# Four rotary layers as one looped program, the next layer's first sequences prepared inside the feed-forward

## The reference, cut to what matters

```python
h = x
for l in range(4):
    xn = _ln(h, ln1_w[l], ln1_b[l])
    q, k, v = heads(xn @ Wq.T + bq), heads(xn @ Wk.T + bk), heads(xn @ Wv.T + bv)
    scores = q @ k.T + rel_shift((q + u) @ pos_emb.T)     # causal mask, times 8 ** -0.5
    h = h + (softmax(scores) @ v) @ Wo.T + bo
    fn = _ln(h, ln2_w[l], ln2_b[l])
    h = h + gelu(fn @ W1.T + b1) @ W2.T + b2              # width 512
```

## Time and profile before

| | us |
|---|---|
| median of 3 runs | 6182.86 (6177.51 to 6191.35) |
| the profiled execution | 6190.3 |
| its span | 6188.5 |
| stage of the four rotary layers, within it | about 2000 to 4732 |

### The profile page before, as it was taken

One profiled execution on the slowest core, in us unless ns is written; L12 is line 12 of the kernel. 1 busy time (PEld: TensorE's weight loads), 2 busy tenths in 40 slices (PEclk: granted clock), 3 DMA queues, 4 the chain that ended last, 5 costly groups with the idle time before them and its releaser, 6 DMA issues. The chain is left out here.

```text
span 6188.5 us, 120583 instructions
## 1 busy us (share of the span) xinstructions
PE 5556.4 (90%) x37438; PEld 3444.4 (56%) x37453; DVE 4189.1 (68%) x9588; ACT 2812.6 (45%) x4608; POOL 2250.4 (36%) x3177
## 2 busy tenths in 40 slices
PE   7997999999998799879988999879988879995677
PEld 5664444444443577547764677447754446644564
DVE  6785666666665788458863788358855866677764
ACT  4553222222222355535554455535555655543444
POOL 5661000000000566236641666246632532253312
PEclk9998999999999899989999999989999989997899
DMA  4332232223223566136530666046520000000002
GB/s 133 106 104 98 97 98 95 95 98 98 94 96 91 149 160 157 40 86 160 157 102 18 160 159 158 9 118 159 157 71 5 0 7 0 0 1 4 0 2 63
DMA packets 526330, 527.02 MB, mean 85 GB/s; under 512 B 55698, under 2 KB 436705, under 8 KB 503780
## 3 DMA queue, kind: packets, MB, share of 16 engines
q1 hardware_dynamic: 517684, 517.90, 30.0%
q10 hardware_dynamic: 8320, 5.25, 0.4%
HBM read 337.88 MB, written 185.07 MB: 85 GB/s over the span
## 5 line engine op out<-in xcount | busy, mean ns | idle before, releaser
L362 DVE TENSOR_REDUCE a_mx<-a_unit 128x2 f32<-128x512 f32 (+1 forms) x1920 | 1291.0, 690 | 413.8 <-PE a_unit L564 407.6
L468 ACT ACTIVATE a_prob<-a_slot 128x1536 f32<-128x1536 f32 x640 | 928.5, 1451 | 643.4 <-PE a_slot L587 505.5
L562 PE MATMUL a_unit<-a_sk,a_sq 96*128 96x256 bf16 (+3 forms) x5120 | 744.9, 249 | 80.3 <-DMA a_sk<-a_kscratch 43.7
L1177 ACT ACTIVATE f_silu<-f_pG 128x512 f32<-128x512 f32 x528 | 314.7, 597 | 937.1 <-PE f_pG L1252 923.1
L564 PE MATMUL a_unit<-a_maskq,identb 128*128 128x256 bf16 (+1 forms) x1920 | 601.7, 313 | 0.0
L1119 DVE TENSOR_TENSOR f_gated<-f_spread,f_silu 128x512 f32<-128x512 f32 x512 | 354.5, 692 | 352.9 <-ACT f_silu L1177 308.7
L1229 PE MATMUL f_pO<-f_hidden,f_wd 128*128 128x512 f32 x1056 | 545.9, 599 | 14.5 <-DVE f_hidden L1121 14.1
L1252 PE MATMUL f_pG<-f_xnT,f_wg 128*128 128x512 f32 x1056 | 542.1, 595 | 0.0
L1256 PE MATMUL f_pU<-f_xnT,f_wu 128*128 128x512 f32 x1056 | 540.7, 594 | 0.0
L562 PEld LDWEIGHTS a_unit<-a_sk,a_sq 96*128 96x128 bf16 (+1 forms) x5120 | 383.7, 98 | 279.4 <-DVE a_mx L362 155.4
L306 POOL TENSOR_SCALAR_AFFINE_SELECT a_prob<-a_prob 128x512 f32<-128x512 f32 x480 | 309.5, 645 | 579.7 <-ACT a_prob L468 564.1
(11 more groups left out here) (413 smaller groups left out, 11144.1 us busy)
## 6 DMA issues: line engine op xcount, KB each, us to landing
f_spread<-f_scratch SPq DMA_DIRECT2D x1024, 128.0 KB, 2.9
a_sq<-a_qscratch SPq DMA_DIRECT2D x128, 768.0 KB, 5.8
a_sk<-a_kscratch SPq DMA_DIRECT2D x160, 384.0 KB, 6.6
a_qscratch<-a_parts SPq DMA_DIRECT2D x288, 192.0 KB, 2.2
a_qscratch<-a_parts SPq DMA_DIRECT2D x288, 128.0 KB, 2.2
a_kscratch<-a_parts SPq DMA_DIRECT2D x160, 192.0 KB, 2.4
a_kscratch<-a_parts SPq DMA_DIRECT2D x160, 128.0 KB, 2.2
a_qscratch<-a_parts SPq DMA_DIRECT2D x288, 64.0 KB, 1.8
```

Of the source, the lines that this page charges most:

```text
L362: v.tensor_reduce(dst, src, op=ALU.max, axis=AX.X, negate=True).then_inc(red_done, 1)
L468: act.activation(prob[gr % 2][:, :], slot[:, :], ACT.Exp, scale=SCALE).then_inc(exp_done, 1)
L562: pe.matmul(bank[:, at * wide:(at + 1) * wide], q, sk[b][0:KM, gr * GH + h, 0:wide], start=(at == 0), stop=False)
L1177: act.activation(silu[c % 2][:, :], pG[c % 2][:, :], ACT.Silu).then_inc(silu_done, 1)
```

## The change

```diff
+    EARLY = {6 + 2 * (n + 5): n for n in range(-5, 0)}
+        pH = [slot[:, c * BLK:(c + 1) * BLK] for c in (0, 1, 2, 1)]
+        pT, pO, pR = unit[0], [unit[1], pctx], ring[0]
...
+    # SyncE
+                attn_weights(0)
+                kept.load(sp, core)
+                feed_weights(0)
+                early_steps()
+                with sp.Fori(1, layers) as following:
+                    main_steps(sp, step)
+                    sp.wait_ge(attn_fresh, 1)
+                    attn_weights(following)
+                    early_steps()
+                    sp.wait_ge(feed_fresh, 1)
+                    feed_weights(following)
+                main_steps(sp, step)
...
+    # GpSimd
+                def feed(following):
+                    for s in range(0, BLOCKS + 1):
+                        if following and s - 2 in EARLY and EARLY[s - 2] > -5:
+                            n = EARLY[s - 2]
+                            gather(n, n // 4, n % 4)
+                            split(n, n % 4)
+                        feed_scale(s)
+                        if following and s == 2:
+                            g.wait_ge(op_taken, SEQS)
+                            g.wait_ge(r_pe, 1)
+                            for x in k.sems:
+                                g.sem_clear(x)
+                            g.sem_inc(attn_fresh, 1)
...
+                    if following:
+                        g.wait_ge(r_taken, BLOCKS)
+                        g.wait_ge(m_pe, 1)
+                        for x in f.sems:
+                            g.sem_clear(x)
+                        g.sem_inc(feed_fresh, 1)
...
+    # VectorE, a round of the feed-forward
+                        feed_norm(s)
+                        if following and s - 1 in EARLY:
+                            norm(EARLY[s - 1])
+                        if s < BLOCKS or not following:
+                            feed_add(s)
+                        v.drain()
+                        feed_measure(s)
...
+                            measure(EARLY[s])
+                        if following and s - 1 in EARLY:
+                            rotate(EARLY[s - 1])
...
+    # ScalarE, step 32
+                    if once(n, SEQS):
+                        act.activation(warm[:, :], core["ident"][:, 0:1], ACT.Gelu)
...
+    # TensorE, a step
+                    maxima(0)
+                    if behind_feed and once(n, -2):
+                        turn_back(BLOCKS)
+                    values(n - 1, (j + 1) % 2, 3)
+                    if once(n, SEQS):
+                        widen(-1, 0)
...
+                    if once(n, SEQS - 1):
+                        pe.wait_ge(red_done, SEQS * UNITS)
+                        pe.wait_ge(w_in, W_IN)
+                        feed_turn(-2)
...
+    # TensorE, a round of the feed-forward
+                        for c in range(CH):
+                            narrow(s, c)
+                            widen(s, c)
+                            if c == 1 and (s < BLOCKS or not following):
+                                turn_back(s)
+                            if c == 1 and following and s in EARLY and EARLY[s] > -5:
+                                turn_rows(EARLY[s])
+                            if c == 2:
+                                feed_turn(s)
+                            if c == 2 and following and s - 1 in EARLY and EARLY[s - 1] > -5:
+                                project_turned(EARLY[s - 1], EARLY[s - 1] % 4)
+                            if c == 3 and following and s in EARLY and EARLY[s] > -5:
+                                project(EARLY[s], EARLY[s] % 4)
```

More of the change, by code:

```diff
@@ L2688, in stage_a1 @@
         kept = Kept(nc, stack, "a1_", True)
[L2689 to L2700, removed]
+        rotary_layers(nc, core, "a1_", core["h"], 1e-6, part_of(a, "a1_"), part_of(a, "f1_"), 4, kept)
         kept.held.clear()
```

685 lines of the change are left out of this document (added).

## The result

The changed kernel takes 6046.7 us (median of 4 runs, 6040.8 to 6048.7), the one before 6183.5 us (4 runs, 6177.5 to 6191.4): ratio 0.9776, 95% interval 0.976 to 0.9793. 6028 was forecast, with a range of 6003 to 6078. Its profiled execution took 6047.05 us, with a span of 6045.3: 143.2 us less than before, where 154.7 were forecast.

The account below looks back on a forecast made before the run. TensorE, busy 90% of the span, bounds the kernel; only the joins, 261 us, leave room. Gains of 107.6 and 52.4 less 3 and 2.3 make 154.7 us, so 6182.9 falls to 6028, range 6003 to 6078.

Parts of the forecast that it names:

- Join from feed-forward to attention: Three joins of 65.0 us: clear, meeting and four sequences' serial start leave; 107.6 us gained, feed-forward's growth and branches included.
- The open steps: Steps -2 and -1 between feed-forward and attention, reduced to 24 units of maxima, still open on the path: 20.0 us.
- The taken branch: Layer loop's branch back between step -1 and step 0, taken twice: 0 to 3.6 us each, 2 assumed.
- Feed-forward: First three layers' feed-forwards take in four sequences' products, 7.8 us more: 127.2 us without TensorE idle time; fourth 119.4.
- The first rival: Feed-forward stretched by its sequences, GpSimd's slack being thin: another 3 us for each of twelve, 6064 us; chance 0.12.
- Join from attention to feed-forward: Four joins of 16.6 us go, 3.5 each comes back in steps 30 to 32: 52.4 us gained.
- step 30's 0.9: Attention's step 30: VectorE's statistics stand ahead of the maxima's parts that TensorE waits for, costing 0.9 us.
- First layer: Start of first layer: four sequences strictly one after another, then 24 units; first scores at about 2076, 3 us lost.
- Second rival: Attention's four-step loop begins to pay for its branch: 16 turns, 51 us, time 6079 us; chance 0.06.
- Third: Rival: early sequences don't overlap in the feed-forward at all; 206 us come back, 6234 us, slower than before; chance 0.03.
- Fourth: Rival: a wait keeps the first maxima back until the fill is as long as now; 6131 us; chance 0.03.
- The likeliest case's own range: 6003 to 6052 us, from bounds on open steps, branches, joins behind attention and start, combined as independent; forecast's chance 0.74.

Follow-up runs that it names:

- the loop of eight: Changed kernel with attention's four-step loop (five passes) made an eight-step loop (two passes), four more steps written out behind it: 6078.4 us, ratio 0.9827 to the kernel before.
- the repeat: The changed kernel timed and profiled once more, no code difference: 6045.0 us, ratio 0.9767 to the kernel before.
- its experiment: Changed kernel with the statistics of the feed-forward's first block moved behind the maxima's parts in attention's step 30: 6033.0 us, ratio 0.9756 to the kernel before.

## Why the prediction was right, point by point

**Join from feed-forward to attention: right, 107.4 us against 107.6, with two errors that cancel.** The open steps were put at 20.0, between the floor of 16.5 (VectorE's reductions) and the ceiling of 26.5. They take 17.0: without norms and rotations nothing but the 24 reductions is left (0.68 us each, where 0.64 was read), so the floor was the estimate to take. That is 9 us too little gain in the forecast. The taken branch was put at 2 us of an open 0 to 3.6. It is 6.6 and 6.3, beyond the bound, which for the two of them makes 9 us too much gain in the forecast; and it has an after-effect of 3 to 4 us each that stands in the attention. That the two errors cancel is luck. The bound came from the old branch, whose place was another: a duration of a branch was taken as its property. The same layer loop's branch takes 3.4 to 3.8 us before, 6.1 to 7.0 in the changed kernel's two profiles and 3.8 to 4.0 with the loop of eight; what sets these sizes is open.

**Feed-forward: right.** Forecast 127.2, measured 127.1, and 119.3 for the fourth. Nothing that SyncE brings is late either: past the after-effect of the branch, the steps behind the join take 15.1 us. The first rival (GpSimd late with the scale, TensorE idle) is false, since TensorE is busy throughout; how much of GpSimd's 1.6 us of slack was left wasn't read.

**Join from attention to feed-forward: 45.4 us against 52.4.** The join went whole, as said. Steps 30 to 32 grew by 3.7 to 5.4 us in the repeat (29.3, 29.2, 29.3 and 30.7 against 25.5, 25.3, 25.6 and 25.3 before); 3.5 were forecast. Of the split of those 3.5, step 30's 0.9 was mis-sized: it grew by 1.8 to 3.4 there, and goes back to within 0.3 us of the old length in its experiment. What remains of the 7 us stands in the layers behind a taken branch, where attention grew by 4.8 and 8.6 (3.1 and 4.1 of it right behind the branch, at half clock), and in single steps that vary from run to run in the kernel before too: its step 29 took 14.2 to 17.1.

**First layer: 3 us lost forecast, 9.6 measured in one profile, 0.9 in the other.** The start was taken as the old one and came out as that: from VectorE's last norm of the stage ahead to its first rotation 28.2 us, 28.8 before. The pitch was right (10.5 against 10.8), and so was the serial order. Of the 9.6 us, 4.3 lie in the stages ahead, in the first profile only; the units were put at 20.0 us and take 17.1 or 21.8 with the clock. What the forecast missed is a gain that was to be had: in that start VectorE waits for the last constant, which is worth 13.9 us.

**The end: 3.2 us against 2.3.** From the last narrowing product to VectorE's first addition of the next stage (answering to the earlier trace rows):

```profile
4583.09 1.88 PE L1325 MATMUL a_pctx<-f_act_out,f_w 128*128 128x512 f32 x4
...
4593.05 0.69 DVE L2177 TENSOR_TENSOR x_store<-x_store,h_store 128x512 f32<-128x512 f32 x1 [5.92 <-PEq L93]
```

VectorE waited 2.75 us, now 5.92: what was forecast as the clear of 47 more semaphores. In GpSimd's stream the clears stand 0.07 us apart and take 4.9 us in all where they took 2.0, so 2.9 of the 3.2; 0.05 each was too low. It wasn't tried apart.

**Second rival, the four-step loop's branch: false here** (0.21 us, the steps at the branches 15.19 to 15.28), and the loop of eight shows that it was a real danger: one doubling of the body, and the price is there. Third: false, since TensorE has no idle time in the feed-forwards, which grow by the products' 7.8 us alone. Fourth: false; the first unit follows the last narrowing product at once.

**The number.** In profiled executions 143.2 us were gained, 11.4 less than forecast: 7.0 in the attention join, 6.6 in the first layer, 0.9 at the end, less 3.2 of drift elsewhere. The other 7 us of the 19 between 6028 and 6046.7 come from the base: the profiled execution before lay 7.4 us above its median, the one after at its median (6047.05 against 6046.7). The sum was made against the one and set against the other. The likeliest case's own range was added up wrongly: its four pairs of bounds, combined as independent, give 6009 to 6055 and not 6003 to 6052. The measured 6046.7 lies in both.

## What to carry to other kernels

A meeting that is removed pays most if the work behind it can be laid beside other work: with the four sequences one behind the other in the open, the longer join was still 57.2 to 65.1 us of 65. When work is taken out of a stretch, read the busy time of the engine that stays (24 x 0.68 us) and take that floor, and price a start by the last of the loads that its first wait names. Count the instructions between a loop's branches on each engine: here a body of 1462 was free on TensorE, one of 2920 cost 3 to 10 us a turn, and writing the layers out gave 13.6 us.

## What the runs showed of the hardware that was not expected

- A taken branch over a whole layer stalls TensorE for 5.8 to 6.6 us in the changed kernel's two profiles, VectorE for 6.0 between its branch and its next instruction. Where TensorE is never idle otherwise, a stall of 3.2 to 3.6 us makes the step 3.4 us longer where the granted clock stays at 1.00 behind it, and up to 9.8 where it falls.
- The same 24 units of maxima take 17 us at a granted clock of 0.92 and 22 us at 0.53, in the same code from one run to the next, at the place that follows TensorE's sparse work.
- Two operations of VectorE on 128x32 take 0.18 and 0.19 us alone and 0.59 and 0.52 us beside GpSimd's selects.
